# Routing weights in eight groups of two units, and 11 more split down units

## Chip, core and metric

The kernel runs on one core of one Trainium2 chip (trn2). The metric is the device time of one execution in microseconds (us); of several runs the median is given. Engines are called PE (TensorE), DVE (VectorE), ACT (ScalarE), POOL (GpSimd) and SP (SyncE, which here only issues transfers).

## What is computed

The reference is a block over x of shape 8 x 512 x 128 (eight sequences of 512 tokens, width 128), all in fp32. A layer norm precedes each step:

```
x = x + attention(ln(x))          # one head, causal
x = x + moe(ln(x))                # 32 experts, top 4 of softmax, plus a shared expert
x = x + rwkv_block(ln(x))         # time mixing with a scan, channel mixing
x = x + moe(ln(x))                # the same weights again
```

and the part that the change is about is, for each of the two moe steps,

```
w[e, token] = softmax weight if expert e is in the token's top 4 and within capacity, else 0
y = sum over e of (silu(x @ W1[e]) * (x @ W3[e]) * w[e]) @ W2[e]     # hidden width 64
z = (silu(x @ Ws1) * (x @ Ws3)) @ Ws2                                 # hidden width 128
```

## The kernel before, in words

**Iterations and units.** The kernel computes all experts densely. Two experts of hidden width 64 fill 128 partitions and form a "unit"; 16 such pairs and the shared expert make 17 units (`UNITS`, 0 to 16). There are 16 iterations g, one for each sequence in each of the two moe steps (g 0 to 7 the first, 8 to 15 the second). In iteration g PE does for each unit p: the gate product into `pa` (`up_gate`), the linear product into `pb` (`up_linear`), and, four units later (`LAG`), the down product into `py` (`out_product`), which accumulates over the 17 units. In between ACT takes silu of `pa` (`unit`, line 732; or tanh with a correction on DVE, lines 734 and 1449, for the units in `TANH`), DVE multiplies by `pb` into `m_v` (`gate`, lines 1468 and 1471), and POOL multiplies by the routing weights `m_wb` into `m_h` (`unit`, line 587). `m_v` has two buffers, `m_h` five.

**Two ways for the down product.** A unit listed in `NATIVE[g]` is done by one fp32 matmul instruction on `m_h` as it stands (line 1067; in the trace it is two records). Any other is "split": ACT rounds `m_h` to the fp32r type into `m_hh` (`split_high`, line 921), DVE or POOL subtracts to get the rest `m_hl` (`split_low`, line 416; POOL where `LOW_ON_POOL` says so, and `LOW_LATE` moves DVE's subtraction behind the gate product of the same slot), and PE does three fp32r matmuls (lines 1072 to 1074). Of 272 down products 88 are native. The up products are always three fp32r matmuls each (lines 1039, 1040, 1043).

**Routing weights.** The routing of sequence q runs one iteration ahead. Its last steps are a transpose on PE (line 1246) and a copy on ACT into `r_wT` (line 823). SP (`spread_weights`) writes `r_wT` to `w_scratch` in DRAM (line 506), waits for that, and loads it back broadcast over 64 partitions for each half of a unit into `m_wb` (line 522). `m_wb` has room for eight units. The loads are in `GROUPS` = 4 groups of `GP` = 4 units, two transfers each, into a ring of `GRING` = 2 groups. A group's load waits until POOL has used up the units whose place it takes; POOL waits once in each group, at its first unit, on that group's semaphore. SP's queue is in order and also holds, at the third group, the transfers in and out of `u_scratch` (`keep`), and the stores of finished sequences. In iteration 0 units 0 and 1 get their weights from PE instead (`spread_step`, `weigh`).

**Order of the work.** Everything else (attention of sequence g+2, time mixing, channel mixing, routing of the next sequence) is put between the units by hand-written tables. Each engine walks slots 0 to 53 of an iteration, three to a unit (PE: gate product, linear product, down product), and a step runs at the slot that its table names for this sequence. An opening of 40 slots (`OPENING`) goes before iteration 0; PE runs 22 filling matmuls there (`keep_clock`, `FILL`). All waits are on semaphores, each engine runs its own queue in order, and no step is dropped or added by moving it to another slot.

Of the kernel before, what the change touches and what calls it, by code (L numbers as in the profile page):

```python
# [21 lines left out]
P = 128  # L22
# [3 lines left out]
T = S // P  # L26
E = 32
H = 64
# [4 lines left out]
GROUPS = 4  # L33
GP = PAIRS // GROUPS
GRING = 2
# [31 lines left out]
    (3, 4, 7, 10, 11, 13, 14, 15),  # L67
    (2, 3, 6, 9, 10, 13, 14),
    (3, 4, 6, 9, 10, 13),
# [5 lines left out]
    (0, 1, 3, 4, 6, 7, 11, 12, 14, 15),  # L75
# [5 lines left out]
    (3, 9, 12, 16),  # L81
# [9 lines left out]
    (0, 1, 3, 6, 7, 10, 13, 14, 15, 16),  # L91
    (0, 2, 4, 7, 9, 10, 16),
    (1, 4, 7, 10, 12),
    (1, 7, 11, 15),
    (2, 4, 10, 12, 13),
    (1, 8, 11, 16),
# [3 lines left out]
    (2, 10, 13, 15),  # L100
    (1, 2, 3, 5, 7, 10, 11),
    (0, 2, 6, 7, 10, 14),
    (0, 1, 6, 8, 11, 13, 15),
# [6 lines left out]
    (0, 1, 6, 8, 11, 14),  # L110
# [9 lines left out]
    (2, 9, 13, 15),  # L120
    (3, 9, 13, 15),
    (1, 5, 11, 12, 16),
    (3, 5, 8),
    (),
# [41 lines left out]
def hybrid_kernel(nc, x_in, att_mats, mats, key_in, vecs, w_gate, w1_in, w3_in, w2_in, x_out):  # L166
    with ExitStack() as ctx:
# [82 lines left out]
        spread = m_y[:, :].rearrange("e (p m) -> e p m", p=GP)  # L250
# [63 lines left out]
        wb_in = [sem(f"s_wb_in{j}") for j in range(GROUPS)]  # L314
# [66 lines left out]
        def last_down(g):  # L381

            return LAST[-1] if g == 2 * B - 1 else UNITS - 1

# [89 lines left out]
        def _(sp):  # L474
# [24 lines left out]
            def spread_weights(q):  # L499
# [8 lines left out]
                for j in range(GROUPS):  # L508
# [36 lines left out]
        def _(pool):  # L545
# [8 lines left out]
            for m in (ident, ident_b):  # L554
# [7 lines left out]
                               pattern=[[P, GP], [1, P]], channel_multiplier=-H).then_inc(sig["c_pool"], 1)  # L562
            pool.wait_ge(sig["c_pool"], 12)
            pool.affine_select(out=spread[:, :, :], in_=spread[:, :, :], compare_op=ALU.is_ge, fill=0.0, base=H - 1,
                               pattern=[[-P, GP], [-1, P]], channel_multiplier=H).then_inc(sig["c_pool"], 1)
# [8 lines left out]
            def unit(g, p):  # L574
# [7 lines left out]
                if p % GP == 0 or (g == 0 and p == SPREAD):  # L582
                    pool.wait_ge(wb_in[p // GP], 32 * g + 32)
# [6 lines left out]
            def att_step(n, slot):  # L590
                if slot == (0, 15, 6, 3, 2, 10, 16, 14)[n]:
                    rsqrt((a_rs if n else a_rq)[:, :], a_ve[:, :], "a_vedone", n + 1, "a_rstd")
# [1309 lines left out]
```

## Time and profile before

| what | value |
|---|---|
| three runs | 793.45, 793.64, 793.45 us (median 793.45) |
| span of the profiled execution, first to last instruction | 791.7 us |
| the profiled execution's own time | not given apart from its span; the median of the runs is 1.75 us above the span |
| busy share PE, DVE, ACT, POOL | 99%, 82%, 72%, 79% |
| granted clock of PE | full (2.4 GHz) in all 40 slices of the page |
| transfers | 80.73 MB, 102 GB/s on average |

The page's busy times count an instruction from its start to its modelled end. PE's matmuls are pipelined and their ends are modelled, so what a matmul costs is read from the distance between the starts of two matmuls, not from the mean duration in the groups. Idle time of an engine is given with what ended it; "issue" there means that the profile shows no releaser.

### The profile page before, as it was taken

The page shows a single profiled execution, that of the slowest core. Times are in us where ns is not written, and L with a number is a line of the kernel's source. Part 1 is how long each engine was busy: PE and PEld are TensorE (multiplying, and loading weights), DVE is VectorE, ACT ScalarE, POOL GpSimd, SP SyncE. Part 2 cuts the span into 40 slices and gives each one's busy share as a digit, 9 for nine tenths or more (in the row PEclk, how much of TensorE's full clock was granted, in tenths as well). Part 3 has the DMA queues.
Part 4 walks back from the last instruction along what each step waited for, and adds up shares of the span by engine and source line. Part 5 has one row for each costly group of instructions (what it writes and reads, how often), then busy time and mean ns, then how long its engine had stood idle before and what let it go on. Part 6 is the DMA issues. An engine that isn't in the chain of part 4 may idle for free.

```text
span 791.7 us, 12780 instructions
## 1 busy us (share of the span) xinstructions
PE 785.1 (99%) x3817; PEld 596.4 (75%) x3817; DVE 645.9 (82%) x1539; ACT 567.9 (72%) x1055; POOL 625.3 (79%) x491
## 2 busy tenths in 40 slices
PE   8999999999999999999999999999999999999998
PEld 5777778676776777768778777887778767788786
DVE  6875577997997989998988869988689889767686
ACT  5677787868768778689765867668685775677553
POOL 6687779849767797769987888998797877876985
PEclk9999999999999999999999999999999999999999
DMA  9353334243144342462425444253444424425552
GB/s 326 95 123 82 87 92 113 66 102 92 42 113 113 73 105 54 110 133 58 120 60 134 104 93 107 65 143 79 110 113 95 90 68 110 111 59 115 124 127 74
DMA packets 49332, 80.73 MB, mean 102 GB/s; under 512 B 3280, under 2 KB 14544, under 8 KB 48880
## 3 DMA queue, kind: packets, MB, share of 16 engines
q1 hardware_dynamic: 48976, 79.72, 42.1%
q8 instruction: 31, 0.51, 0.3%
q14 instruction: 37, 0.30, 0.1%
q10 hardware_dynamic: 288, 0.20, 0.1%
HBM read 75.19 MB, written 4.72 MB: 101 GB/s over the span
## 4 chain that ended last, share of the span: by engine, by line
PE 51%; POOL 2%; issue 2%; DVE 1%; ACT 0%; DVEq 0%; POOLq 0%; ACTq 0%
PE pa L1039 5%; PE pb L1039 4%; PE py L1067 4%; PE pa L1043 4%; PE pb L1043 4%; PE pa L1040 4%; PE pb L1040 4%; PE pu L1326 4%; PE py L1072 3%; PE py L1074 3%; PE py L1073 3%; POOL m_h L587 1%; PE pq L1283 1%; PE pu L1310 1%; PE pv L1334 1%
## 5 line engine op out<-in xcount | busy, mean ns | idle before, releaser
L587 POOL TENSOR_TENSOR m_h<-m_v,m_wb 128x512 f32<-128x512 f32 x254 | 364.3, 1444 | 98.7 <-DVE m_v L1468 42.9
L732 ACT ACTIVATE m_th<-pa 128x512 f32<-128x512 f32 x220 | 130.6, 594 | 102.0 <-PE pa L1043 97.7
L1468 DVE TENSOR_TENSOR m_v<-m_th,pb 128x512 f32<-128x512 f32 x205 | 138.6, 679 | 23.9 <-ACT m_th L732 15.5
L1039 PE MATMUL pa<-m_xh,w1h 128*128 128x512 f32 x272 | 137.2, 504 | 0.3 <-DVE m_v L1471 0.2
L416 DVE TENSOR_TENSOR m_hl<-m_h,m_hh 128x512 fp32r<-128x512 f32 x120 | 111.4, 929 | 24.8 <-ACT m_hh L921 24.1
L921 ACT ACTIVATE m_hh<-m_h 128x512 fp32r<-128x512 f32 x184 | 115.2, 626 | 13.8 <-POOL m_h L587 13.1
L1039 PE MATMUL pb<-m_xh,w3h 128*128 128x512 f32 x272 | 115.4, 424 | 0.0
L1043 PE MATMUL pa<-m_xl,w1h 128*128 128x512 f32 x272 | 107.3, 394 | 0.3 <-POOL m_xl L608 0.3
L1043 PE MATMUL pb<-m_xl,w3h 128*128 128x512 f32 x272 | 107.1, 394 | 0.0
L1040 PE MATMUL pa<-m_xh,w1l 128*128 128x512 f32 x272 | 106.6, 392 | 0.0
L1040 PE MATMUL pb<-m_xh,w3l 128*128 128x512 f32 x272 | 106.5, 391 | 0.0
L416 POOL TENSOR_TENSOR m_hl<-m_h,m_hh 128x512 fp32r<-128x512 f32 x64 | 86.1, 1345 | 12.6 <-ACT m_hh L921 12.1
L1072 PE MATMUL py<-m_hh,w2h 128*128 128x512 f32 x183 | 77.2, 422 | 0.0
L1074 PE MATMUL py<-m_hl,w2h 128*128 128x512 f32 x183 | 72.0, 394 | 0.0
L1073 PE MATMUL py<-m_hh,w2l 128*128 128x512 f32 x183 | 71.6, 392 | 0.0
L1039 PEld LDWEIGHTS pa<-m_xh,w1h 128*128 128x128 f32 x272 | 51.5, 189 | 25.5 <-issue 14.4
L1040 PEld LDWEIGHTS pa<-m_xh,w1l 128*128 128x128 f32 x272 | 51.5, 189 | 20.6 <-issue 14.6
L1039 PEld LDWEIGHTS pb<-m_xh,w3h 128*128 128x128 f32 x272 | 51.3, 189 | 14.0 <-issue 3.9
L1043 PEld LDWEIGHTS pa<-m_xl,w1h 128*128 128x128 f32 x272 | 51.1, 188 | 12.2 <-POOL m_xl L608 0.7
L1043 PEld LDWEIGHTS pb<-m_xl,w3h 128*128 128x128 f32 x272 | 51.1, 188 | 11.6
L1040 PEld LDWEIGHTS pb<-m_xh,w3l 128*128 128x128 f32 x272 | 51.4, 189 | 10.8 <-issue 1.9
L1449 DVE SCALAR_TENSOR_TENSOR m_th<-m_th,pa 128x512 f32<-128x512 f32 x52 | 35.2, 677 | 15.9 <-ACT m_th L734 15.8
(318 smaller groups left out, 1653.8 us busy)
## 6 DMA issues: line engine op xcount, KB each, us to landing
m_wb<-w_scratch SPq DMA_DIRECT2D x126, 512.0 KB, 6.5
x_sb<-in_x SPq DMA_DIRECT2D x8, 256.0 KB, 7.2
m_wb<-in_w SPq DMA_DIRECT2D x2, 1024.0 KB, 6.8
x_out<-x_sb SPq DMA_DIRECT2D x7, 256.0 KB, 6.6
u_scratch<-t_u SPq DMA_DIRECT2D x6, 256.0 KB, 2.6
t_u<-u_scratch SPq DMA_DIRECT2D x6, 256.0 KB, 2.7
f_kk<-in_w SPq DMA_DIRECT2D x1, 1024.0 KB, 9.7
w_scratch<-r_wT SPq DMA_DIRECT2D x16, 64.0 KB, 1.5
```

Of the source, the lines that this page charges most:

```text
L416: eng.tensor_tensor(m_hl[:, at, :], hidden(g, p), m_hh[:, at, :].bitcast(F32), ALU.subtract)\
L587: pool.tensor_tensor(hidden(g, p), gated(g, p), m_wb[:, p % (GRING * GP), :], ALU.mult).then_inc(sig["m_h"], 1)
L732: ins = act.activation(m_th[:, p % 2, :], pa[p % 2][:, :], ACT.Silu)
L921: act.activation(m_hh[:, halves_at(g, p), :], hidden(g, p), ACT.Copy).then_inc(sig["m_hh"], 1)
L1039: pe.matmul(ps[:, :], high[:, p, :], xh, start=True, stop=False)
L1040: pe.matmul(ps[:, :], low[:, p, :], xh, start=False, stop=False)
L1043: return pe.matmul(ps[:, :], high[:, p, :], xl, start=False, stop=True)
L1072: pe.matmul(py[:, :], w2h[:, p, :], hh, start=(p == 0), stop=False)
L1073: pe.matmul(py[:, :], w2l[:, p, :], hh, start=False, stop=False)
L1074: pe.matmul(py[:, :], w2h[:, p, :], hl, start=False, stop=(p == last_down(g))).then_inc(sig["m_y"], 1)
L1449: dve.scalar_tensor_tensor(out=m_th[:, r, :], in0=m_th[:, r, :], scalar=1.0, in1=pa[r][:, :], op0=ALU.add, op1=ALU.mult).then_inc(sig["m_u ...
L1468: dve.tensor_tensor(gated(g, p), m_th[:, r, :], pb[r][:, :], ALU.mult).then_inc(sig["m_v"], 1)
```

## The change

It sets `GROUPS` to 8 and `GRING` to 4, so that a group is two units (`GP` = 2) and the ring still holds eight units. The group semaphores are now four, one for each place of the ring, and POOL waits for its group at every even unit with a count worked out by a new function `weights_in`. Iteration 0 no longer loads group 0 (units 0 and 1). Eleven entries leave `NATIVE`; a few entries of `LOW_ON_POOL`, `LOW_LATE` and `TANH` change; and most entries of the slot tables of all four engines are new. The core of the diff (tables of which only the numbers change are cut after a few that the text speaks of):

```diff
-GROUPS = 4
+GROUPS = 8
 GP = PAIRS // GROUPS
-GRING = 2
+GRING = 4
...
 NATIVE = (
     (3, 9),
     (11,),
-    (2, 3, 5, 6, 9, 10, 11, 12, 13),
-    (1, 2, 3, 4, 5, 7, 9, 10, 11, 12, 13, 14, 15),
+    (2, 3, 5, 6, 9, 11, 12, 13),
+    (1, 3, 5, 7, 10, 11, 12, 13, 14, 15),
     (3, 5, 6, 7, 9, 10, 11, 13, 16),
-    (1, 2, 7, 9, 10, 11, 12, 13),
-    (1, 3, 5, 7, 9, 15),
+    (1, 7, 9, 10, 12, 13),
+    (1, 3, 7, 9, 15),
     (1, 5, 7, 9, 11),
     (1, 3, 5, 7, 9, 11, 16),
-    (1, 3, 5, 7, 9),
-    (3, 5, 7, 9, 11, 15),
+    (1, 5, 7, 9),
+    (3, 5, 7, 9, 11),
     (1, 7, 9, 11, 16),
-    (3, 7, 9, 11, 13, 15),
-    (3, 7),
+    (3, 7, 9, 11, 15),
+    (7,),
...
-        wb_in = [sem(f"s_wb_in{j}") for j in range(GROUPS)]
+        wb_in = [sem(f"s_wb_in{j}") for j in range(GRING)]
...
+        def weights_in(g, j):
+
+            return 32 * (GROUPS // GRING * g + j // GRING + (0 if j % GRING == 0 else 1))
...
-                for j in range(GROUPS):
+                for j in range(1 if q == 0 else 0, GROUPS):
...
                     if j >= GRING:
                         sp.wait_ge(sig["m_h"], PAIRS * q + GP * (j - GRING + 1))
                     elif isinstance(q, int) and q == 0:
 
-                        sp.wait_ge(sig["c_wl"], 2 * QUARTERS - 1 + j)
+                        sp.wait_ge(sig["c_wl"], 2 * QUARTERS - 1 + 2 * j // GRING)
                     else:
                         sp.wait_ge(sig["m_h"], PAIRS * (q - 1) + GP * (GROUPS - GRING + j + 1))
                     if j == GRING:
                         keep(plan(q))
                     at = GP * (j % GRING)
-                    first = SPREAD if q == 0 and j == 0 else 0
                     for h in range(2):
-                        sp.dma_start(m_wb[H * h:H * (h + 1), at + first:at + GP, :],
-                                     w_scratch[q, j, first:GP, h, :].partition_broadcast(H)).then_inc(wb_in[j], 16)
+                        sp.dma_start(m_wb[H * h:H * (h + 1), at:at + GP, :],
+                                     w_scratch[q, j, :, h, :].partition_broadcast(H)).then_inc(wb_in[j % GRING], 16)
...
-                if p % GP == 0 or (g == 0 and p == SPREAD):
-                    pool.wait_ge(wb_in[p // GP], 32 * g + 32)
+                if p % GP == 0:
+                    pool.wait_ge(wb_in[p // GP % GRING], weights_in(g, p // GP))
...
# ACT, the copy into r_wT (line 823), by sequence q
-                if slot == (37, 43, 41, 43, 43, 43, 42, 43, 43, 43, 44, 44, 44, 47, 42, 39)[q]:
+                if slot == (37, 44, 45, 44, 53, 48, 45, 48, 45, 48, 40, 49, 47, 53, 53, 42)[q]:
...
# PE, the transpose before it (line 1246), by sequence q
-                if slot == (31, 44, 41, 44, 42, 44, 42, 44, 45, 47, 45, 46, 44, 47, 46, 39)[q]:
+                if slot == (27, 43, 46, 45, 47, 46, 43, 45, 43, 48, 41, 47, 46, 49, 46, 42)[q]:
```

## Rows read from the trace of the kernel before

**Rows 1.** The page, part 1: busy us (share of span) and instructions of each engine.

```profile
PE 785.1 (99%) x3817; PEld 596.4 (75%) x3817; DVE 645.9 (82%) x1539; ACT 567.9 (72%) x1055; POOL 625.3 (79%) x491
```

**Rows 2.** Busy by stretch: opening, iterations 0 to 15, tail; clock, DMA share, GB/s last.

```profile
0.00:24.17 24.17, 21.93 (x120) 1.00 0.89 291
24.17:784.71 760.54, 759.32 (x3681) 1.00 0.41 97
784.71:791.70 6.99, 3.89 (x20) 1.00 0.13 38
...
170.68:221.52 50.84, 50.84 (x243) 36.59 (x241) 43.87 (x109) 37.82 (x70) 39.73 (x30) 1.00 0.44 103
272.82:323.53 50.71, 50.71 (x242) 37.25 (x241) 45.92 (x109) 38.91 (x73) 41.35 (x32) 1.00 0.46 103
565.04:612.05 47.01, 46.47 (x230) 35.87 (x229) 41.21 (x89) 30.19 (x56) 38.23 (x28) 1.00 0.50 117
```

**Rows 3.** The chain that ended last, from 740 us on: start us, us, what.

```profile
744.02 0.23 PE py L1072
746.08 0.86 PE py L1067 x2
748.78 0.23 PE py L1074
786.81 0.23 PE py L1073
```

**Rows 4.** Groups of instructions: form, count | busy us, mean ns | idle before, releasers.

```profile
L921 ACT ACTIVATE m_hh<-m_h 128x512 fp32r<-128x512 f32 x184 | 115.2, 626 | 13.8 <-POOL m_h L587 13.1
L416 DVE TENSOR_TENSOR m_hl<-m_h,m_hh 128x512 fp32r<-128x512 f32 x120 | 111.4, 929 | 24.8 <-ACT m_hh L921 24.1
L416 POOL TENSOR_TENSOR m_hl<-m_h,m_hh 128x512 fp32r<-128x512 f32 x64 | 86.1, 1345 | 12.6 <-ACT m_hh L921 12.1
L1449 DVE SCALAR_TENSOR_TENSOR m_th<-m_th,pa 128x512 f32<-128x512 f32 x52 | 35.2, 677 | 15.9 <-ACT m_th L734 15.8
```

**Rows 5.** DMA issues: KB each, median us from issue to landing.

```profile
m_wb<-w_scratch SPq DMA_DIRECT2D x126, 512.0 KB, 6.5
m_wb<-w_scratch SPq DMA_DIRECT2D x2, 256.0 KB, 3.8
w_scratch<-r_wT SPq DMA_DIRECT2D x16, 64.0 KB, 1.5
```

**Rows 6.** Line 522 on SP (ns min/median/max), and SP's own waits (us, times, longest).

```profile
L522 SPq DMA_DIRECT2D m_wb<-w_scratch x128: 573/602/1382, 33.0 to 769.6; - x128
...
SPq L522 <- POOL m_h L587: 263.0, 38, 14.1
SPq L506 <- ACT r_wT L823: 255.1, 15, 22.1
SPq L496 <- DVE t_u L1741: 32.2, 3, 12.7
```

**Rows 7.** What POOL waited for before line 587: us in total, times, longest.

```profile
POOL m_h L587 <- DVE m_v L1468: 42.9, 29, 4.8
POOL m_h L587 <- issue: 26.0, 18, 5.6
POOL m_h L587 <- DMA m_wb<-w_scratch: 12.3, 5, 3.1
```

**Rows 8.** Head of iteration 11, timelines of SP, POOL, ACT, DVE, PE: start us, us.

```profile
560.77 0.33 SPq L506 DMA_DIRECT2D w_scratch<-r_wT  x1
562.31 3.97 SPq L522 DMA_DIRECT2D m_wb<-w_scratch  x4
571.04 4.25 POOL L587 TENSOR_TENSOR m_h<-m_v,m_wb 128x512 f32<-128x512 f32 x3 [3.05 <-DMA m_wb<-w_scratch]
561.64 0.60 ACT L732 ACTIVATE m_th<-pa 128x512 f32<-128x512 f32 x1
566.76 0.69 DVE L1468 TENSOR_TENSOR m_v<-m_th,pb 128x512 f32<-128x512 f32 x1
585.11 0.42 PE L1218 MATMUL pv<-t_v,wg 128*32 128x128 f32 x8 [0.34 <-ACT m_xh L808]
```

**Rows 9.** Head of iteration 14, timelines of ACT, SP, POOL and PE: start us, us.

```profile
705.31 0.26 ACT L823 ACTIVATE r_wT<-pq 128x128 f32<-128x128 f32 x1
710.64 0.62 ACT L921 ACTIVATE m_hh<-m_h 128x512 fp32r<-128x512 f32 x1
...
705.60 0.33 SPq L506 DMA_DIRECT2D w_scratch<-r_wT  x1
707.34 4.08 SPq L522 DMA_DIRECT2D m_wb<-w_scratch  x4
...
714.81 1.62 POOL L587 TENSOR_TENSOR m_h<-m_v,m_wb 128x512 f32<-128x512 f32 x1 [2.18 <-DMA m_wb<-w_scratch]
...
711.33 0.39 PE L1039 MATMUL pa<-m_xh,w1h 128*128 128x512 f32 x1
721.30 0.48 PE L1072 MATMUL py<-m_hh,w2h 128*128 128x512 f32 x1
721.62 0.40 PE L1073 MATMUL py<-m_hh,w2l 128*128 128x512 f32 x1
721.86 0.39 PE L1074 MATMUL py<-m_hl,w2h 128*128 128x512 f32 x1
```

More of the change, by code:

```diff
@@ L80 @@
     (12, 13, 14, 16),
-    (3, 9, 12, 16),
+    (3, 9, 11, 12, 16),
 )
@@ L666, in channel_step @@
             def channel_step(m, slot):
-                if slot == (40, 36, 38, 43, 41, 38, 44, 23)[m]:
+                if slot == (31, 38, 38, 40, 36, 36, 43, 41)[m]:
                     kept(pool, m)
@@ L737, in att_step @@
             def att_step(n, slot):
-                if slot == (0, 11, 13, 10, 19, 19, 23, 19)[n]:
+                if slot == (0, 15, 14, 10, 22, 22, 25, 22)[n]:
                     if n > 0:
@@ L825, in time_begin @@
             def time_begin(m, slot, q):
-                if slot == (13, 9, 12, 11, 10, 9, 10, 7)[m]:
+                if slot == (10, 9, 12, 11, 13, 9, 9, 7)[m]:
                     vectors_loaded()
@@ L930, in first_step @@
             def first_step(slot):
-                if slot == (33,)[0]:
+                if slot == (36,)[0]:
                     unit(0, 0)
-                if slot == (37,)[0]:
+                if slot == (36,)[0]:
                     unit(0, 1)
@@ L1095, in att_step @@
             def att_step(n, slot, n_chunk, n_chunk_in_pv):
-                if slot == (1, 13, 19, 15, 28, 23, 28, 26)[n]:
+                if slot == (2, 14, 19, 20, 26, 27, 28, 26)[n]:
                     if n == 1:
@@ L1125, in att_step @@
                     ins.then_inc(sig["a_vps"], 1)
-                if slot == (1, 18, 23, 30, 35, 30, 36, 36)[n]:
+                if slot == (2, 14, 24, 32, 33, 33, 36, 33)[n]:
                     if n == 0:
@@ L1249, in spread_step @@
             def spread_step(slot):
-                if slot == (34,)[0]:
+                if slot == (31,)[0]:
                     pe.wait_ge(sig["r_wT"], 1)
@@ L1262, in time_begin @@
                     turn(pq, t_hn, "t_tr")
-                if slot == (27, 28, 28, 25, 28, 29, 24, 25)[m]:
+                if slot == (27, 28, 28, 25, 28, 25, 24, 25)[m]:
                     if m in MIXED:
@@ L1287, in time_out @@
             def time_out(m, slot, q):
-                if slot == (9, 11, 6, 5, 7, 11, 0, 10)[m]:
+                if slot == (4, 10, 6, 6, 8, 13, 2, 6)[m]:
                     pe.wait_ge(sig["t_rw"], m + 1)
@@ L1306, in channel_step @@
                     key(m, 0, pv)
-                if slot == (36, 42, 32, 42, 35, 41, 38, 42)[m]:
+                if slot == (35, 42, 33, 41, 38, 41, 28, 43)[m]:
                     pe.wait_ge(sig["f_xk"], 2 * m + 2)
@@ L1482, in att_step @@
             def att_step(n, slot):
-                if slot == (0, 7, 8, 1, 1, 11, 9, 13)[n]:
+                if slot == (0, 4, 7, 2, 1, 11, 8, 10)[n]:
                     if n < 2:
@@ L1516, in weights_step @@
                     high_part(w2h[:, 0:PAIRS, :], w2_stage, "in_w2")
-                if slot == (35,)[0]:
+                if slot == (32,)[0]:
                     high_part(w1h[:, PAIRS, :], mt[:, M_S1, :], "in_mt")
@@ L1523, in weights_step @@
                     low_part(w2l[:, PAIRS, :], mt[:, M_S2, :], w2h[:, PAIRS, :], 6)
-                if slot == (39,)[0]:
+                if slot == (36,)[0]:
                     high_part(key_h[:, :], key_stage, "in_key")
@@ L1565, in pro_step @@
             def pro_step(q, slot, cmix):
-                if slot == (16,)[0] and q == 0:
+                if slot == (19,)[0] and q == 0:
                     dve.wait_ge(sig["a_add"], 2)
@@ L1685, in fold_step @@
             def fold_step(slot):
-                if slot == (42,)[0]:
+                if slot == (21,)[0]:
                     dve.wait_ge(sig["in_vec"], 16)
@@ L1693, in time_finish @@
             def time_finish(m, slot):
-                if slot == (42, 43, 35, 35, 12, 12, 2, 48)[m]:
+                if slot == (42, 43, 34, 35, 10, 12, 1, 47)[m]:
                     dve.wait_ge(sig["t_ev"], m + 1)
@@ L1737, in time_out @@
             def time_out(m, slot):
-                if slot == (10, 12, 12, 8, 9, 11, 5, 17)[m]:
+                if slot == (10, 9, 11, 13, 7, 10, 5, 16)[m]:
                     dve.wait_ge(sig["t_ops"], m + 1)
```

316 lines of the change are left out of this document (158 added, 158 removed).

## Prediction

> **What bounds the kernel.** The page's first part says which engine is full: PE 99%, DVE 82%, POOL 79%, ACT 72% [rows 1]. A share over the whole span could hide stages with other limits, so the span is cut into stretches next [rows 2]. Opening: PE idle 24.17 - 21.93 = 2.2 us. All 16 iterations up to the last down products: 760.54 - 759.32 = 1.2 us. Tail: 3.1 us. So through 96% of the span PE never stands still, at full clock, while POOL waits often [rows 7] and nobody on the path waits for it. Idle time of POOL is not to be had; what can be had is PE's own work, the 1.2 us, and part of the opening. Third, the chain of waits, which in the iterations is PE behind PE, gives the true price of a matmul, because it counts start to start: a native down product is 0.86 us (two records), each of the three matmuls of a split one 0.23 us [rows 3].
>
> **The change part by part.**
>
> *11 more split units* (88 native before, 77 after: one less in iterations 2, 6, 9, 10, 12, 13, three less in 3, two in 5). PE: 0.86 - 3 x 0.23 = 0.17 us saved each, 11 x 0.17 = **-1.9 us**, and as PE is the path it counts in full. ACT gets 11 roundings, 11 x 0.626 = 6.9 us. By the tables DVE's subtractions go from 120 to 129 and POOL's from 64 to 66: 9 x 0.929 = 8.4 us and 2 x 1.345 = 2.7 us. Three more tanh units add 3 x 0.677 = 2.0 us on DVE [rows 4]. All this lies beside PE, which takes a down product four units after its gate; I cost it at nothing. The cover is thinnest on DVE: 43.87 of 50.84 us in iteration 3 and 45.92 of 50.71 in iteration 5 [rows 2]; with three and two subtractions more they stand at 46.7 and 47.8 us, 92% and 94%. Without cover these five would cost up to 4.6 us. Below zero it cannot go.
>
> *Groups of two.* Bytes are the same; the transfers are 254 of 256 KB instead of 126 of 512 and 2 of 256. SP issues 126 more at 0.602 us, 76 us, and spends 263 + 255 us waiting for POOL and ACT anyway [rows 6]; it is no bound. Behind a waiting SP are the later loads: the `keep` transfers now stand before the fifth group of two (units 8 and 9), after unit 1 is weighed, instead of before the third group of four (after unit 3). Their longest wait is 12.7 us for a result of DVE. Eight units are loaded by then, six of them not yet used, at 47.01 / 17 = 2.8 us a unit [rows 2] some 17 us; nothing. POOL waits at 127 places instead of 64; its gate products stand behind each wait, DVE (two buffers of `m_v`) and ACT behind those. The loads are due six units ahead, 17 us, against a landing of 6.5 us before [rows 5]. So inside an iteration these waits cost zero, and the 12.3 us that POOL waits for transfers, with an unknown part of the 26.0 put down to "issue" [rows 7], were mostly free already.
>
> Where a group is late is the **head of an iteration**, since the routing ends only just before. There the first pair of 512 KB has landed 0.6 + 6.5 = 7.1 us after its issue; two of 256 KB take 0.6 + 3.8 = 4.4 [rows 5, 6], a gain of 2.7 us. The 3.8 is from two transfers only; the bounds are 0 and 3.6 (half of 7.1). I take 2.7, as the row is of the very size. The Trainium skill ("DMA: Bandwidth & Descriptors", section Bandwidth and the cost components ahead of it) speaks against halving: some 2.0 us fixed for each transfer plus bytes at 436 GB/s, and batch towards 1 MiB. By that 512 KB would take 3.2 us and 256 KB 2.6, and the gain would be 0.6 us; the trace has 6.5 and 3.8, so here the part that grows with size is the larger.
>
> *The routing's last step moves later.* ACT's copy to `r_wT` goes from slot 43 to 53 for sequence 4, 47 to 53 for 13, 42 to 53 for 14, and by one to five for eleven others (40 and not 44 for 10), so part of the gain is spent. Head 14 is the sharpest. Its copy ran at 705.31. At slot 53 it follows the last rounding of iteration 13, which ends at 710.64 + 0.62 = 711.26: 6.0 us later. The write is issued 0.3 later, the loads 1.7 after that (the write's median is 1.5, [rows 5]), landing 4.4 on: 717.7, where POOL before began unit 0 at 714.81 when its weights had come [rows 9]. So POOL is 6.0 - 2.7 = 3.3 us late. What is due next is the down product of unit 0, at 721.30; from 714.81 on, the product (1.62), the rounding (0.63) and the subtraction (0.93) take until 717.99, a slack of 3.3 us [rows 4, 9]. The lateness just fits. For queueing behind other steps I put 0.1 us on each of heads 4, 13, 14: **+0.3 us**; bounds 0 and 2.7 each (no gain from smaller transfers: 6.0 - 3.3).
>
> At head 11 POOL waited 3.05 us for its weights until 571.04, though DVE's product had been there since 567.45; and in this iteration PE stood still for 47.01 - 46.47 = 0.5 us, 0.34 of it at 585.11 [rows 2, 8]. Its copy moves from slot 44 to 49, behind the silu that ends at 562.24; the write had been issued at 560.77. That is some 1.8 us later against 2.7 gained, and this pair was slower than the median. Between 0 and 0.5 I take all: **-0.5 us**.
>
> *All other moved steps.* None is added or dropped, and PE's count of slots with an inserted step goes from 218 to 216. They move past each other on four engines, and the only prize is PE's idle time: bounds -1.2 (the iterations') and -1.1 (half of the opening's 2.2) on one side, and as much idle time once more, +2.3, on the other. In the opening the eight low parts of the weights and the first routing steps keep nearly their order on POOL. I take 0. The tail's own tables (last three down products, the one by token) don't change; 0.
>
> **Sum.** -1.9 - 0.5 + 0.3 = -2.1 us. On the profiled span: 791.7 - 2.1 = 789.6. The runs' median lies 1.75 us above the span, carried over unchanged: **791.4 us**. A measurement of this kernel can tell about 0.2%, 1.6 us, from no change; so "faster" begins below 791.9, and the forecast is only just beyond it.
>
> **Rivals.**
>
> *A. The helpers eat the gain.* DVE at 92 to 94% in iterations 3 and 5 comes late with `m_hl` or `m_v`. For: these were its fullest stretches. Against: PE had no idle time there before [rows 2], and four units of lag. At half the price of the five subtractions, 2.3 us: 793.45 - 1.9 + 2.3 = 793.8; with less, between this and 791.9. No change.
>
> *B. Late weights, slower.* The small transfers land no sooner than the large ones, while the copies to `r_wT` have moved. Head 14 then loses 2.7 us; heads 4 and 13, taken at half of that, 2.7 together: 793.45 - 1.9 + 5.4 = 797.0. It decides once the three heads lose 3.5 us together, that is when the gain of a pair is below about 1 us. Against: the 3.8 us row. By the Trainium skill's figures (same page) the gain would be 0.6 us, and this case would come about.
>
> *C. More comes back.* PE's idle in iterations and half of the opening go: -1.9 - 1.2 - 1.1 = -4.2, 789.2 us.
>
> *D. DVE becomes the bound* in iterations 3, 5 and 12: price of all added there, 6 x 0.93 = 5.6 us, 797.2 us.
>
> **Numbers.** Forecast 0.49, C 0.08, A 0.25, B 0.13, D 0.05. Faster 0.57, within 0.2% 0.25, slower 0.18. The range goes down to C, 789.2, and up to most of B, 795.6, which leaves out the upper part of B and D.
>
> **What would show it.** Right: 77 x 2 native records instead of 88 x 2 (some records can be missing), still 0.86 and 0.23 us in the chain; PE idle from the first unit to 784 or so at most 1.5 us; m_wb transfers of 256 KB landing in about 3.8 us; POOL's first product of iteration 14 about 3 us later against PE's first gate product (3.5 us after it before). Wrong: pairs landing in 6 us or more; PE idle of over 2 us after the heads of iterations 4, 13 or 14 (B); PE waiting for `m_hl` or `m_v` of DVE in iterations 3 or 5 (A, D); an opening whose first gate product starts more than 1 us off 24.17.

## The result, and the profile after

The changed kernel took **793.76 us** (median of 20 executions, 793.08 to 797.58) against 793.13 us (20, 792.52 to 794.13) for the kernel before: ratio 1.0015, interval 1.0009 to 1.0022. That is slightly slower, inside the 0.2% counted as no change, and 2.4 us above the forecast of 791.4. The profiled execution of the changed kernel took 793.08 us, the lowest of its 20 times, with a span of 791.3; the span of before is 791.7. Of 28 executions of the changed kernel, in two sets, 12 had a mean granted clock of PE of 0.996 to 0.998 and took 794.7 to 797.6 us, the other 16 (0.999 or 1.0) 793.1 to 795.1.

The page, part 1, after (against [rows 1]):

```profile
PE 782.9 (99%) x3828; PEld 598.4 (76%) x3828; DVE 655.4 (83%) x1551; ACT 569.0 (72%) x1062; POOL 635.1 (80%) x493
```

Eleven native products became 33 matmuls for 22 records, so PE has 11 instructions more and is busy 2.2 us less. Stretches of the changed kernel, columns as in [rows 2] (start:end and length in us, then the busy time of each engine, clock, DMA share, GB/s): opening, iteration 0, iterations 1 to 15, then iterations 3, 5 and 11:

```profile
0.00:27.54 27.54, 23.19 (x127) 1.00 0.78 256
27.54:77.29 49.75, 49.23 (x259) 1.00 0.33 82
77.29:784.33 707.04, 706.61 (x3430) 1.00 0.40 98
172.89:224.32 51.43, 51.11 (x246) 37.12 (x244) 45.35 (x111) 37.35 (x74) 38.87 (x28) 1.00 0.33 84
275.30:325.90 50.60, 50.60 (x247) 37.31 (x245) 46.63 (x112) 37.08 (x72) 42.65 (x32) 1.00 0.36 90
567.00:612.70 45.70, 45.70 (x233) 36.29 (x232) 40.64 (x91) 32.64 (x59) 36.12 (x27) 1.00 0.48 112
```

The kernel before:

```profile
24.17:75.50 51.33, 51.06 (x265) 1.00 0.37 88
75.50:784.71 709.21, 708.26 (x3417) 1.00 0.42 97
```

**Where gain and loss sit.** From the head of iteration 1 (its first gate product) on, the change gains 709.21 - 707.04 = 2.2 us, about the forecast's sum. But the opening is 27.54 - 24.17 = 3.4 us longer. It holds seven PE instructions more and iteration 0 six fewer, and iteration 0 is 1.6 us shorter, so 1.8 us of loss are left at the head of iteration 1. Together the two give the -0.4 us between the spans. The medians say +0.6, because the execution profiled here is the fastest of its 20; a second profile of the changed kernel, from an execution of 793.84 us, has the head of iteration 1 at 77.88, where the loss is 2.4 us.

One pair of profiles is not exact to better than 1 us, the gain included. From the head of iteration 1 to the end, four profiles with the iterations of before take 714.9 to 716.2 us (the kernel before and the second, third and seventh experiment), and seven with those of the change 713.1 to 715.3. Nor does the 2.2 us sit where the forecast had it. Iterations 11 and 12 are shorter by 1.3 and 0.8 us, where it had 0.5 and 0.2, and iteration 3, with three split units more, is 0.6 us longer instead of 0.5 shorter (51.43 against 50.84). The profile of before has 47.01 and 52.90 us for iterations 11 and 12; other profiles of the same iterations go down to 45.99 and 52.41. So this sum came right in part by luck; the medians of the fifth and sixth experiment are the better evidence of the gain.

The chain, the groups and the transfers answer to the terms of the sum. From the chain of the changed kernel, as [rows 3], then the groups, as [rows 4], then the transfers, as [rows 5]:

```profile
744.01 0.23 PE py L1076
745.84 0.86 PE py L1070 x2
```

```profile
L924 ACT ACTIVATE m_hh<-m_h 128x512 fp32r<-128x512 f32 x195 | 122.0, 626 | 11.8 <-POOL m_h L590 11.5
L420 DVE TENSOR_TENSOR m_hl<-m_h,m_hh 128x512 fp32r<-128x512 f32 x129 | 117.7, 914 | 23.1 <-ACT m_hh L924 22.1
L420 POOL TENSOR_TENSOR m_hl<-m_h,m_hh 128x512 fp32r<-128x512 f32 x66 | 89.0, 1348 | 10.2 <-ACT m_hh L924 9.9
```

```profile
m_wb<-w_scratch SPq DMA_DIRECT2D x254, 256.0 KB, 4.4
```

The matmuls cost what they did before, 0.23 and 0.86 us, and the counts are as worked out (195, 129, 66). A 256 KB transfer lands in 4.4 us where [rows 5] had 3.8 for two of them.

**Where the opening lost.** DVE's timeline from 6 us on, changed kernel (start us, us, instruction, in brackets the idle time before it and what ended it), then the kernel before:

```profile
7.11 1.11 DVE L1443 TENSOR_SCALAR a_xn<-x_sb,a_q,a_rq 128x128 f32<-128x128 f32 x4 [1.14 <-POOL a_rq L575]
10.35 0.87 DVE L1419 BATCH_NORM_STATS2 a_st<-x_sb 128x6 f32<-128x128 f32 x4 [2.12 <-DMA x_sb<-in_x]
11.14 1.21 DVE L1534 CAST w1h<-m_wb 128x2048 fp32r<-128x2048 f32 x1
12.75 0.61 DVE L1544 TENSOR_REDUCE a_nm<-pv 128x1 f32<-128x128 f32 x2
```

```profile
8.29 1.22 DVE L1531 CAST w1h<-m_wb 128x2048 fp32r<-128x2048 f32 x1
10.57 0.62 DVE L1541 TENSOR_REDUCE a_nm<-pv 128x1 f32<-128x128 f32 x2 [1.06 <-PE pv L1158]
13.15 0.86 DVE L1416 BATCH_NORM_STATS2 a_st<-x_sb 128x6 f32<-128x128 f32 x4
```

Before, the layer norm statistics of sequence 1 (`att_step`, n = 1) stood behind the row maxima of sequence 0's first attention, and started when DVE was free. Now they stand in front of the rounding of W1 and of the maxima, and they need sequence 1's `x`, which has not landed: DVE's queue stands 2.12 us, and the maxima come at 12.75, not 10.57. When that load lands could be read in the profile of before, from the line of SP that issues it (start and time to landing):

```profile
L478 SPq DMA_DIRECT2D x_sb<-in_x x1: 433/433/433, 2.3 to 2.3; - x1
DMA to landing us min/median/max: 8.2/8.2/8.2
```

Issued at 2.3 us, it was in at 10.5. ACT's exponential and PE's transpose follow, changed kernel first, then the exponential of before:

```profile
13.77 0.46 ACT L787 ACTIVATE a_p<-pv,a_nm,a_rq 128x128 f32<-128x128 f32 x1 [2.35 <-DVE a_nm L1552]
```

```profile
15.01 0.52 PE L1176 MATMUL pb<-ident,a_p 128*128 128x128 f32 x3 [1.47 <-ACT a_p L787]
```

```profile
11.60 0.46 ACT L784 ACTIVATE a_p<-pv,a_nm,a_rq 128x128 f32<-128x128 f32 x1 [0.77 <-DVE a_nm L1549]
```

2.2 us on DVE are 2.2 us on ACT, and PE stands still for 1.47 of them. Theories at this point: **T1**, the opening's order on DVE (and what it pulls along) is the whole loss, and the rest of the forecast holds; **T2**, the opening is longer for another reason (start-up, more work moved in) and the gain is really eaten by split units' helpers or late weights. In each set of experiments the kernel before ran again on the same chip (medians 793.43, 793.48, 793.27, 793.28); ratios are against those. The changed kernel itself ran again only beside the ninth and tenth experiment; a difference from its first 793.76 in another experiment is one between chips.

### The profile page after: what moved, and what is told of

Same layout as the page of the kernel before. It is cut to its first block, busy times and chain, and to the rows that moved or that the text cites. A ratio compares the mean times of both kernels' runs of the same rounds, so it can differ in the third digit from the quotient of the medians.

```text
span 791.3 us, 12964 instructions
## 1 busy us (share of the span) xinstructions
PE 782.9 (99%) x3828; PEld 598.4 (76%) x3828; DVE 655.4 (83%) x1551; ACT 569.0 (72%) x1062; POOL 635.1 (80%) x493
## 4 chain that ended last, share of the span: by engine, by line
PE 96%; DVE 1%; DMA 1%; ACT 1%; issue 1%; SPq 0%; DVEq 0%
PE py L1070 8%; PE pa L1042 8%; PE pb L1042 8%; PE pa L1046 8%; PE pb L1046 8%; PE pa L1043 8%; PE pb L1043 8%; PE py L1075 6%; PE py L1077 6%; PE py L1076 5%; PE pu L1329 4%; PE pq L1286 2%; PE pu L1186 2%; PE pv L1160 2%; DMA x_sb<-in_x 1%; PE pu L1313 1%
## 5 line engine op out<-in xcount | busy, mean ns | idle before, releaser
L590 POOL TENSOR_TENSOR m_h<-m_v,m_wb 128x512 f32<-128x512 f32 x254 | 372.1, 1473 | 90.0 <-issue 36.9
L735 ACT ACTIVATE m_th<-pa 128x512 f32<-128x512 f32 x217 | 128.5, 593 | 95.4 <-PE pa L1046 91.3
L420 DVE TENSOR_TENSOR m_hl<-m_h,m_hh 128x512 fp32r<-128x512 f32 x129 | 117.7, 914 | 23.1 <-ACT m_hh L924 22.1
L1042 PE MATMUL pa<-m_xh,w1h 128*128 128x512 f32 x272 | 134.3, 494 | 0.1
L924 ACT ACTIVATE m_hh<-m_h 128x512 fp32r<-128x512 f32 x195 | 122.0, 626 | 11.8 <-POOL m_h L590 11.5
L1042 PE MATMUL pb<-m_xh,w3h 128*128 128x512 f32 x272 | 117.0, 430 | 0.2 <-DVE m_v L1471 0.2
L420 POOL TENSOR_TENSOR m_hl<-m_h,m_hh 128x512 fp32r<-128x512 f32 x66 | 89.0, 1348 | 10.2 <-ACT m_hh L924 9.9
L1075 PE MATMUL py<-m_hh,w2h 128*128 128x512 f32 x194 | 83.2, 429 | 0.0
L1077 PE MATMUL py<-m_hl,w2h 128*128 128x512 f32 x194 | 76.2, 393 | 0.0
L1076 PE MATMUL py<-m_hh,w2l 128*128 128x512 f32 x194 | 75.8, 391 | 0.0
L737 ACT ACTIVATE m_th<-pa 128x512 f32<-128x512 f32 x55 | 32.4, 592 | 23.0 <-PE pa L1046 22.8
```

Source lines behind the costliest of these rows:

```text
L420: eng.tensor_tensor(m_hl[:, at, :], hidden(g, p), m_hh[:, at, :].bitcast(F32), ALU.subtract)\
L590: pool.tensor_tensor(hidden(g, p), gated(g, p), m_wb[:, p % (GRING * GP), :], ALU.mult).then_inc(sig["m_h"], 1)
L735: ins = act.activation(m_th[:, p % 2, :], pa[p % 2][:, :], ACT.Silu)
L924: act.activation(m_hh[:, halves_at(g, p), :], hidden(g, p), ACT.Copy).then_inc(sig["m_hh"], 1)
L1042: pe.matmul(ps[:, :], high[:, p, :], xh, start=True, stop=False)
L1075: pe.matmul(py[:, :], w2h[:, p, :], hh, start=(p == 0), stop=False)
```

## Experiments

### The statistics put back alone

```diff
# DVE att_step of the changed kernel: statistics, then moments
-                if slot == (0, 4, 7, 2, 1, 11, 8, 10)[n]:
+                if slot == (0, 7, 7, 2, 1, 11, 8, 10)[n]:
-                if slot == (2, 5, 7, 3, 3, 11, 15, 14)[n]:
+                if slot == (2, 7, 7, 3, 3, 11, 15, 14)[n]:
```

> The changed kernel, with only DVE's statistics and moments of sequence 1 put back behind the three maxima of sequence 0 in the opening (slot 7 for both, instead of slots 4 and 5). Theory 1 (in the opening DVE now waits 2.1 us for the load of sequence 1 in front of everything else): the wait goes, the maxima start about 2 us earlier (10.7 instead of 12.75 us), the first gate product starts near 25.5 us instead of 27.5, and the time falls by 1.5 to 2 us against the changed kernel, to about 792.0, below the kernel before. Rival, late weights at the heads of the iterations: the opening gets shorter but the time stays at 793.5 or more, because the loss is elsewhere. Rival, the opening's length is absorbed in iteration 0: the head of iteration 1 stays at 77.3 us and the time does not move.

Measured 795.34 us (794.41 to 796.9, 10), ratio 1.0026 (1.0016 to 1.0035): not 792 but slower than the changed kernel, though the supposed cause was gone. All ten executions had a mean granted clock of 0.996 to 0.998, so what this order takes at full clock was not measured. Its timeline of POOL, its timeline of PE, and its windows of 2 us (us, PE busy, PEclk, DMA share, GB/s):

```profile
15.58 1.02 POOL L575 TENSOR_TENSOR a_q<-a_ve,minus_half 128x4 f32<-128x4 f32 x1 [4.58 <-DVE a_ve L1434]
19.23 3.78 POOL L646 TENSOR_TENSOR w1l<-m_wb,w1h 128x512 fp32r<-128x512 f32 x3
22.97 1.01 POOL L575 TENSOR_TENSOR r_q<-r_ve,minus_half 128x4 f32<-128x4 f32 x1
```

```profile
24.41 1.10 PE L990 MATMUL pq<-ident,t_k 128*128 128x128 f32 x4 [1.56 <-DVE t_k L1443]
```

```profile
26.00:28.00 2.00, 1.56 (x11) 0.88 0.03 8
28.00:30.00 2.00, 2.00 (x6) 0.50 0.00 0
```

On POOL the change had also moved the inverse root of sequence 1 from slot 15 to 8, ahead of the weights' low parts. With the statistics late again, POOL stood 4.58 us for them with `w3l` and `w1l` behind, the first routing came late, PE stood still for 1.56 us, and its granted clock then fell to 0.50 (1.2 GHz). First gate product: 29.54. Read so, DVE's slots and POOL's belong together, and one cannot be judged with the other in place; the ninth experiment tests that.

### The statistics put forward in the kernel before

```diff
# DVE att_step of the kernel before
-                if slot == (0, 7, 8, 1, 1, 11, 9, 13)[n]:
+                if slot == (0, 2, 8, 1, 1, 11, 9, 13)[n]:
-                if slot == (0, 7, 9, 1, 2, 11, 17, 13)[n]:
+                if slot == (0, 2, 9, 1, 2, 11, 17, 13)[n]:
```

> The kernel before, with the same two steps moved the other way (statistics and moments of sequence 1 at slot 2, ahead of the rounding of W1 and of the maxima). Theory 1: DVE idles some 2 us until the load of sequence 1 is in (near 10.3 us), the head of iteration 1 moves from 75.5 to about 77.5, and the time rises by 1.5 to 2 us, to about 795. Rivals (the opening is covered, or the loss of the change is elsewhere): under 0.5 us, 793.1 to 793.6.

Measured 797.18 us (796.19 to 797.34, 5), ratio 1.0049 (1.0035 to 1.0063), twice the loss expected. DVE's timeline of this kernel and PE's waits in its opening (us in total, times, longest):

```profile
10.66 0.87 DVE L1416 BATCH_NORM_STATS2 a_st<-x_sb 128x6 f32<-128x128 f32 x4 [2.12 <-DMA x_sb<-in_x]
13.30 0.62 DVE L1541 TENSOR_REDUCE a_nm<-pv 128x1 f32<-128x128 f32 x2
```

```profile
PE pb L1173 <- ACT a_p L784: 2.5, 1, 2.5
PE pa L987 <- ACT a_xn L904: 0.9, 1, 0.9
```

The same 2.12 us of idle time, and 797.18 - 793.43 = 3.75 us for a layer norm's statistics and moments that nobody needs early. The first of these waits is not there in the kernel before and the second is 0.3 us, so they account for 3.1 us, and the head of iteration 1 comes 3.3 us later (78.78). This direction of the mechanism is shown by itself. The other, taking the step back out of the changed kernel, failed above and works only together with POOL's slots (below).

### Groups of two alone

```diff
# the kernel before, with the changed kernel's group code (loads, waits, weights_in)
-GROUPS = 4
+GROUPS = 8
-GRING = 2
+GRING = 4
```

> The kernel before, all its tables kept, with the routing weights in eight groups of two units. Theory 1 and the forecast: pairs of 256 KB land about 2.7 us earlier at the heads, the idle 0.5 us at the head of iteration 11 goes (start to start it was about 1.1), nothing else moves: -0.5 to -1.2 us, 792.0 to 792.6. Rival (63 more waits on POOL and 126 more transfers cost time by themselves, or small transfers land no sooner): no gain, or up to +2 us, 793.1 to 795.

Measured 792.95 us (792.18 to 793.85, 11), ratio 0.9997 (0.9988 to 1.0006): no difference that can be told. Its window of iteration 11:

```profile
565.03:611.20 46.17, 46.16 (x231) 35.90 (x229) 41.44 (x89) 29.95 (x56) 39.11 (x28) 1.00 0.50 123
```

Iteration 11 is 0.84 us shorter than in [rows 2], which looks like my term of -0.5. It cannot be put down to the groups: see iteration 11 of the seventh experiment.

### Split units alone

```diff
# the kernel before, with NATIVE, LOW_ON_POOL, LOW_LATE and TANH of the changed kernel; iteration 3:
-    (1, 2, 3, 4, 5, 7, 9, 10, 11, 12, 13, 14, 15),
+    (1, 3, 5, 7, 10, 11, 12, 13, 14, 15),
```

> The kernel before, groups of four kept and slots kept, with the changed kernel's four unit tables (11 more split, LOW_ON_POOL, LOW_LATE, TANH). If the price of 0.17 us a unit holds and the helpers have room: -1.9 us, about 791.3. If the new subtractions and roundings come late without the rest of the plan (the rival of the helpers): between 0 and -1 us, or slower, with PE idle seen in iterations 3 and 5.

Measured 806.91 us (805.68 to 808.5, 4), ratio 1.0173 (1.0158 to 1.0188). Windows of iterations 3 and 5, and PE's longest waits behind the opening (us in total, times, longest):

```profile
173.14:228.76 55.62, 51.75 (x245) 36.70 (x244) 48.78 (x111) 39.31 (x73) 39.95 (x30) 1.00 0.39 92
280.52:334.00 53.48, 51.35 (x245) 37.11 (x243) 47.61 (x111) 39.84 (x75) 41.38 (x32) 1.00 0.40 94
```

```profile
PE pu L987 <- ACT a_xn L904: 1.9, 3, 1.2
PE pu L1183 <- ACT a_pT L792: 1.5, 2, 1.3
PE pq L987 <- DVE t_u L1741: 1.5, 1, 1.5
PE pv L1157 <- ACT a_p L784: 1.5, 1, 1.5
```

In the old places of the inserted steps the four tables cost 13.5 us: iteration 3 goes from 50.84 to 55.62. The eleven roundings and subtractions are most of what they add to ACT and DVE; they were not tried apart from the three tanh units more and the moved subtractions. PE hardly waits for `m_hh` or `m_hl` themselves (once, 0.6 us). It waits for attention and time mixing steps that stand behind them on ACT and DVE. These are rival D's places (iterations 3, 5 and 12), at 4.8 + 2.8 + 1.2 = 8.8 us where D had 5.6, and the changed kernel, with its new slots and groups of two, does not have them (iteration 5: 50.60).

### The natives of before in the changed kernel

```diff
# changed kernel; eight rows of NATIVE as before, for instance
-    (1, 3, 5, 7, 10, 11, 12, 13, 14, 15),
+    (1, 2, 3, 4, 5, 7, 9, 10, 11, 12, 13, 14, 15),
```

> The changed kernel with the 88 native units of before (table NATIVE alone). If the price of 0.17 us a unit holds and the helpers are no bound: +1.8 us of PE's work, less what PE stands still in iterations 2 and 3 now (0.9 us by start to start), so 794.5 to 795.6. If the 11 split units cost PE more than they save (rival of the helpers): at or below the changed kernel, 793.8 or less.

Measured 795.73 us (795.65 to 797.43, 5), ratio 1.0039 (1.0027 to 1.0052): 2.0 us above the changed kernel of the first result, where the forecast had 1.9 for these eleven. But iteration 3 alone is 1.1 us longer in its profile (52.55 against 51.43), where three units at 0.17 would be 0.5. The rest may be slots that were made for other lengths; no run tells it apart from chance.

### The opening of before in the changed kernel

```diff
# changed kernel; entries n = 0, 1 of the attention tables, q = 0 of time mixing and routing,
# and the weights' steps, on PE, DVE, ACT and POOL, as before the change; on DVE for instance
-                if slot == (0, 4, 7, 2, 1, 11, 8, 10)[n]:
+                if slot == (0, 7, 7, 2, 1, 11, 8, 10)[n]:
```

> The changed kernel, with all of the opening's tables (steps of attention 0 and 1, routing 0, the weights' rounding and low parts, the first two units) as they were before; iterations, groups of two and 77 native units stay. Theory 1, widened after the first runs (the change's new opening as a whole costs 1.8 us up to the head of iteration 1, and its idle time lets PE's clock fall in some executions): first gate product near 24.2 us, head of iteration 1 near 75.5, mean granted clock 1.0 in all executions, and the median 2 to 3 us below the changed kernel, 790.8 to 791.8, where the forecast for the whole change was. Rival, late weights or late helpers in the iterations: the time stays within 1 us of the changed kernel.

Measured **791.24 us** (790.2 to 792.89, 11), ratio 0.9976 (0.9967 to 0.9985). This is the value of T1, as widened after the first four experiments to the whole opening, and the forecast's (791.4), 2.2 us below the kernel before on the same chip, and all eleven executions had a granted clock of 0.999 or 1.0. Its opening and iteration 0, in the profile of its slowest execution (792.89):

```profile
0.00:24.92 24.92, 22.67 (x121) 15.05 (x121) 15.38 (x67) 13.58 (x34) 13.44 (x26) 1.00 0.86 283
24.92:75.90 50.98, 50.71 (x266) 38.55 (x265) 37.45 (x120) 37.22 (x75) 42.14 (x36) 1.00 0.32 81
```

The head of iteration 1 is at 75.90, where it was at 75.50 before and at 77.29 with the change.

### The new opening in the kernel before

```diff
# kernel before; the same entries as in the changed kernel
-                if slot == (0, 7, 8, 1, 1, 11, 9, 13)[n]:
+                if slot == (0, 4, 8, 1, 1, 11, 9, 13)[n]:
```

> The kernel before, with the changed kernel's opening tables alone. Theory 1: head of iteration 1 near 77.3 instead of 75.5, time 1.8 us up at full clock (795.2), and some executions at a mean granted clock of 0.998 or less with 1 to 3 us more; median 795 to 796. Rival: no change, 793.4.

Measured 797.36 us (796.2 to 797.87, 5), ratio 1.0046 (1.0033 to 1.006); 2 us more than expected. In three of five the mean granted clock was 0.997 or 0.998; the other two took 796.2. In the profiled one PE stood still from 14 to 16 us and was granted 1.2 GHz from 18 to 20 us:

```profile
18.00:20.00 2.00, 2.00 (x12) 2.00 (x10) 0.00 (x0) 1.44 (x4) 2.00 (x2) 0.50 1.20 291
```

Its iteration 11 settles another point. The code there is that of before, with groups of four:

```profile
570.17:616.16 45.99, 45.99 (x231) 35.89 (x229) 41.12 (x89) 30.10 (x56) 38.27 (x28) 1.00 0.52 120
```

45.99 us where [rows 2] have 47.01 for the same instructions. The 0.5 us of idle time that I gave to the groups is there or not with groups of four as well.

### Groups of four in the changed kernel

```diff
# changed kernel, with the group code of before
-GROUPS = 8
+GROUPS = 4
-GRING = 4
+GRING = 2
```

> The changed kernel with the routing weights again in four groups of four; all tables of the changed kernel kept, so the copies into r_wT stay late. If the groups of two are what pays for the later copies (forecast: gain of 2.7 us in landing, slack 3.3 at head 14): PE idle appears behind the heads of iterations 4, 13 and 14, 1 to 2.7 us at 14, together 2 to 6 us, so 795.5 to 799. If the moved copies have more slack than worked out: under 1 us, 793.5 to 794.8.

Measured 817.48 us (816.83 to 819.89, 4), ratio 1.0311 (1.0295 to 1.0327), where I expected at most 799. All four had a mean granted clock of 0.994 to 0.997, so a part that was not measured is the clock's. POOL's waits before the routing weights are used, this kernel first, then the changed kernel (us in total, times, longest):

```profile
POOL m_h L591 <- DMA m_wb<-w_scratch: 60.8, 14, 7.1
```

```profile
POOL m_h L590 <- DMA m_wb<-w_scratch: 24.7, 9, 4.7
```

At the heads a pair of 512 KB transfers lands 7.1 to 8.0 us after its first issue, a pair of 256 KB in the changed kernel 4.9. With groups of four and the late copies to `r_wT`, POOL is late at almost every head, up to 7.1 us, and PE waits behind it (iteration 6: 55.25 us against 49.80). So the groups of two, worth nothing by themselves, carry the new slots: 24 us in their absence. The fear of rival B was right in kind; with the groups of two it does not come about.

### Statistics and POOL's opening back

```diff
# changed kernel; DVE as in the first experiment, and POOL's opening of before, for instance
-                if slot == (3, 8, 6, 1, 4, 10, 16, 14)[n]:
+                if slot == (0, 15, 6, 1, 4, 10, 16, 14)[n]:
```

> The changed kernel; in the opening the statistics and moments of sequence 1 on DVE are put back as in e1, and POOL's opening tables (all low parts, both inverse roots, routing 0) are those of before. PE's, ACT's and the rest of DVE's new opening stays. Theory 1a (the loss is this pair: DVE waits for sequence 1's load in front of the maxima, and if that is mended alone, as in e1, POOL's inverse root of sequence 1 stands in front of four low parts and they come late): first gate product near 25 to 26 us, clock 1.0, median 791 to 792, nearly as good as e6. Rival 1b (the order on PE and ACT costs as much): stays at 793 or more.

Measured 792.61 us (791.91 to 793.28, 11), ratio 0.9991 (0.9982 to 1.0). With POOL's slots back as well, the statistics' return takes 1.2 us off the changed kernel's 793.76, and 2.5 off its 795.06 on the same chip (below). So the first experiment failed for POOL's slots, as read there; which of POOL's entries it was is not tried. Two things are left. Five of the eleven executions had a mean granted clock of 0.997 or 0.998, as the profiled one; there PE was busy for 1.29 of the 2 us from 22 us on and for 1.78 of the next, and then came this window:

```profile
26.00:28.00 2.00, 2.00 (x6) 0.50 0.00 0
```

And the six at full clock have a median of 792.1, still 0.8 us above the experiment with all of DVE's and POOL's opening back (791.33, below): the other new entries of DVE's opening probably cost something too, if the two chips compare (the kernel before takes 793.27 and 793.28 on them).

### More filling matmuls

```diff
# changed kernel, PE's filling matmuls by slot
-FILL = (8, 1, 0, 1, 4, 2, 0, 2, ...
+FILL = (8, 1, 0, 1, 4, 8, 0, 2, ...
```

> The changed kernel with six more filling matmuls (8 instead of 2) on PE where it waits some 1.5 us for the first probabilities in the opening. They end before what PE waits for, so nothing gets later. Theory (the executions above 794.4 us are those in which PE's idle time in the opening is followed by a stretch at 1.2 GHz): mean granted clock 1.0 in all executions, none above 794.5, median 793.0 to 793.7. Rival (the slow executions come from late transfers): spread of executions as before, 793.1 to 797.6.

Measured 793.53 us (792.57 to 794.51, 11), ratio 1.0006 (0.9998 to 1.0015), in all eleven with a granted clock of 0.999 or 1.0. PE's timeline has the fill in the place of a part of the wait:

```profile
12.21 2.11 PE L980 MATMUL pq<-ones_b 128*128 128x512 bf16 x9
15.29 0.52 PE L1176 MATMUL pb<-ident,a_p 128*128 128x128 f32 x3 [0.97 <-ACT a_p L787]
```

### The changed kernel once more

> The changed kernel itself, on the chip of the two runs beside it, so that these can be compared with it: 793.1 to 793.8 us in the executions at a mean granted clock of 1.0, 794.4 to 797.6 in the others, about a third of them.

On the same chip as the last two it took 795.06 us (793.48 to 795.92, 8), ratio 1.0024 (1.0014 to 1.0035). Six of eight, not a third, had a granted clock of 0.998 and took 794.7 or more; the two at 1.0 took 793.48 and 793.84. With six more filling matmuls none of eleven executions fell, and the median is that of the ones at full clock here. So the new opening has a second cost, 1 to 4 us in the executions with a lower clock (against 793.6), and in this kernel the fills in front of the wait at 15 us take it away. The wait at 15 us is not its only occasion: in the ninth experiment, where PE does not stand there, the clock fell in five of eleven.

### DVE's and POOL's opening back, PE's and ACT's new

```diff
# changed kernel; all opening entries of DVE and POOL as before the change, for instance
-                if slot == (3, 8, 10, 9, 9, 15, 21, 20)[n]:
+                if slot == (2, 10, 10, 9, 9, 15, 21, 20)[n]:
```

> The changed kernel with the opening tables of before on both DVE and POOL; PE's and ACT's opening tables stay those of the change. It tells where the rest of the opening's loss sits, between the kernel with only the statistics and POOL's steps back (792.61 us, some 792.0 at full clock) and the one with all opening tables back (791.24). If the loss is all on DVE and POOL: 791.0 to 791.8 us, first gate product at 24.2 to 25.5, head of iteration 1 at 75.5 to 76.2. If PE's and ACT's own new order carries the rest: 791.9 to 792.8, like the former. If the tables of the four engines only fit together (PE's new slots ask DVE for steps in the new order): over 793, with idle time of PE before products of the first routing or attention.

Measured **791.33 us** (791.11 to 792.66, 11), ratio 0.9982 (0.9972 to 0.9991), all at 1.0: the same as with the whole opening back (791.24). The loss sits on DVE and POOL; the new order on PE and ACT costs nothing that can be measured. The first gate product is at 26.05, later than expected, but the head of iteration 1 is at 76.24. The eleven times fall into two heaps, six from 791.11 to 791.33 and five from 792.04 to 792.66. Only one of them was profiled (791.11), and it shows something that could make such heaps. Iteration 3 takes 50.53 us here, 51.43 in the changed kernel, by the same instructions. DVE's and POOL's timelines at the place, changed kernel:

```profile
177.26 1.82 DVE L420 TENSOR_TENSOR m_hl<-m_h,m_hh 128x512 fp32r<-128x512 f32 x1
177.24 1.29 POOL L590 TENSOR_TENSOR m_h<-m_v,m_wb 128x512 f32<-128x512 f32 x1 [2.94 <-issue]
```

and this kernel:

```profile
176.21 0.69 DVE L420 TENSOR_TENSOR m_hl<-m_h,m_hh 128x512 fp32r<-128x512 f32 x1
176.21 1.85 POOL L590 TENSOR_TENSOR m_h<-m_v,m_wb 128x512 f32<-128x512 f32 x1 [2.94 <-issue]
```

The two start within 0.02 us of each other. One takes its usual time (0.69 on DVE, 1.29 on POOL), the other nearly its own and the partner's together (1.82 and 1.85, against a sum of 1.98). Where DVE is the one held up, its next `m_v` is 1.1 us late, and PE stands still. Of eight profiles with these two instructions at this distance, DVE was held up in seven (1.80 to 1.83 us), with POOL's start on record 0.01 to 0.03 us before its own, and POOL in this one alone. Whether the slower heap is the same race was not seen. A held-up subtraction is no proof of idle PE time either: just before the idle time of iteration 11 in [rows 8], DVE's took 1.65 us at 584.51, with POOL's product running from 584.33, but the seventh experiment has the same row and no idle time in that iteration:

```profile
588.67 1.60 DVE L416 TENSOR_TENSOR m_hl<-m_h,m_hh 128x512 fp32r<-128x512 f32 x1 [0.89 <-ACT m_hh L921]
```

## Why the prediction was wrong

**The step that failed** is "All other moved steps ... In the opening the eight low parts of the weights and the first routing steps keep nearly their order on POOL. I take 0." I looked at POOL's low parts and at the count of PE's slots, and not at DVE, where the statistics of sequence 1 went from slot 7 to 4. The bound that I wrote (-1.2 to +2.3) held the 1.8 us of the profile; the value taken did not. What the runs showed in its place: with all of the opening's tables put back the kernel takes 791.24 us, with DVE's and POOL's alone 791.33, so this term is some +2.4 us and not 0 (2.9 if each kernel is taken against the kernel before on its own chip, +0.6 and -2.2). Inside it, the sentence on POOL was wrong as well: the inverse root of sequence 1 crossed from slot 15 to 8, and the low parts, four of `w1l` in a row before, now have that root and one of `w3l` between them. The row needed was in the trace of before: the load of sequence 1's `x` landed at 10.5 us. How much of it the statistics have alone is not shown; in the kernel before they cost 3.75. I priced the opening's steps by what is idle and not by what each waits for, which is what the timeline of DVE would have told at once. The last sign of being wrong in the prediction, an opening more than 1 us off 24.17, is what came (27.54).

The forecast missed by 2.4 us: 1.7 in the profiled span (791.3 and not 789.6) and 0.7 because the median lies 2.5 us above that span and not 1.75, as the profile is of the fastest execution.

**-1.9, split units.** Right in the matmuls: 0.23 and 0.86 us in the chain. Right in sum by the fifth experiment, where 11 fewer natives are worth 2.0 us (on another chip); the 2.2 us of the one pair of profiles are partly luck, as said above. "I cost it at nothing" (the helpers) holds only with the new slots and the groups of two; by itself it costs 13.5 us. Here I named DVE as the cover and iterations 3 and 5 as the place, which was right; but who waits is not the down product four units on but the other chains behind the helpers, so the lag of four units does not protect those. Rival D did not happen, and rival A in iteration 3 alone: in seven of eight profiles DVE is held up there, and the changed kernel's iteration is 0.9 us longer than that of the eighth profile (51.43 against 50.53), though by POOL holding up one subtraction and not by DVE being full.

**-0.5, the head of iteration 11.** Not shown. The groups alone measure 0.9997 (0.9988 to 1.0006), and the idle time is absent in one profile with groups of four. It was a term read from a single profile.

**+0.3, later copies.** Nothing of it is seen: iteration 14 takes 37.44 us after and 37.52 before. Two sizes were off. A pair of transfers gains 7.3 - 4.9 = 2.4 us (I had 2.7, from the 3.8 us of two transfers, median now 4.4). And the write at head 14 comes 2.55 us later against the head, not 6.0: I put the old time of the last rounding into the new slot, though what stands before that slot had moved too. POOL's first product then starts 3.39 us after the head instead of 3.48, where I wanted 3 us later. The Trainium skill ("DMA: Bandwidth & Descriptors", section Anatomy of one DMA) has a fit of 2.0 us plus bytes at 436 GB/s, measured on transfers that GpSimd issues. By it the estimated gain would be 0.6 us, and with it rival B; these transfers, issued by SP and broadcast, took 6.5 and 4.4 us and do not agree, and the eighth experiment shows what the two sizes are worth.

**Rivals.** None of the four came with its price. That 793.76 is rival A's 793.8 is luck: A has 2.3 us lost in iterations 3 and 5, where the profiles show 0.9 in iteration 3, and the kernel with the old opening has that loss too and takes 791.24. The case that did come, a new wait in the opening, was only a bound of a term and not a rival with a price; its place was on the list of what would prove me wrong. With the opening undone the forecast holds to 0.2 us (791.24), so the mechanism of the main term was right and the verdict, faster, wrong.

## What to carry over

A step that is moved earlier in an in-order queue must be checked for what it waits for, a load above all: everything behind it is then late by that wait. An engine's share of busy time in a stretch says nothing of this; list for each moved step its last input, and do it in the opening first, where inputs arrive from outside. A gain of 0.1 to 1 us at one place of one profile is not a term: look for it in a second profile, and look whether two engines start together there, before it is ascribed to a cause.

## What was not expected of the hardware

**The start of PE differs between executions.** The first filling matmuls start 0.43 us apart, later ones 0.21 to 0.22, and the moment of the change differs between executions of the same instructions. Timeline of PE at the start, kernel before, then changed kernel:

```profile
5.30 0.60 PE L987 MATMUL pu<-ident,x_sb 128*128 128x128 f32 x4
```

```profile
5.86 0.99 PE L990 MATMUL pu<-ident,x_sb 128*128 128x128 f32 x4
```

By the distance from each matmul to the next, the last start at the slow pace is at 4.16 us before, at 6.29 and 7.14 in two executions of the changed kernel, at 3.73 in the last experiment, while the granted clock of these stretches is given as 1.00. Two openings with the same tables on all four engines, in the kernel before and in the sixth experiment (last slow start 6.72), differ by 24.92 - 24.17 = 0.75 us, and by 0.4 us at the head of iteration 1. So up to that much of the 3.4 us, and of the 1.8, may be chance and no cost of the change. The Trainium skill ("TensorE: Matmul & The Clock Gate", section Part 1: The HAM clock gate) says that the number of slow matmuls at a kernel's start varies from run to run; these traces agree, with 6.29 and 7.14 us in the same kernel, and it should have been in my reading of 24.17.

**DVE and POOL starting together**, above: one of them is held up by the other, it is not always the same one, and here it moves an iteration by 0.9 us. The Trainium skill ("SBUF — State Buffer", section SBUF: two separate sides) has the rule that DVE, with two inputs from SBUF, and GpSimd take a shared port pair by turns and the later one is blocked for the whole instruction. The four rows above agree (0.69 and 1.85, or 1.82 and 1.29); what was new is how close the race is.

**The two costs of the opening** can be told apart by the clock. The changed kernel's 14 executions at 0.999 or 1.0 have a median of 793.64, so of the first 793.76 the lower clock has 0.1 us and the late steps the rest of the loss; in the second set, with six of eight fallen, the clock has 1.4 of its 795.06.

**Left open:** why an idle PE is followed by 1.2 GHz in some executions and not in others, and how the late steps' cost divides between the statistics and the other moved entries of DVE and POOL. Other places where DVE and POOL meet were not tried.
